# A transformer block on eight cores: the casts of two weight matrices are spread, and drained, at other places of the queue

## The chip, the cores and the metric

The kernel runs on the 8 cores of one Trainium2 chip. Each core does the whole block for its own 1,024 tokens; the cores exchange nothing. The time is that of the slowest core on the device, in microseconds (us). Engines are called as the profile does: PE (TensorE), DVE (VectorE), ACT (ScalarE), POOL (GpSimd), SP (SyncE).

## What is computed

```
x: 2 x 4096 tokens, 4096 wide, float32;  Wq, Wo: 4096 x 4096;  K, V: 8 heads x 8192 keys x 128 (gathered)
def ffn(x):    # 8 low-rank experts, rank 16, routed by a softmax
    scores = 8 * softmax(x @ Wr.T + br)
    low = einsum('bsd,hrd->bshr', x, A)
    return 2 * einsum('bshr,hor,bsh->bso', low, B, scores)
def attn(x):   # 32 query heads, 8 K/V heads, rope on q, no mask
    q = rope(x @ Wq)
    return softmax(q @ K.T / sqrt(128)) @ V @ Wo
x = x + 0.5 * ffn(layernorm(x))
x = x + attn(layernorm(x))
x = x + 0.5 * ffn(layernorm(x))
```

## The kernel before

A core takes its tokens in two chunks of 512 (c = 0 and 1), and the stages of a chunk follow each other: LN, FFN, LN, QT (q with rope), ATT, WO, LN, FFN, STORE. Activations lie transposed in SBUF, 32 tiles of 128 x 512: X in float32, XN and QC in bf16. The program writes one list of instructions for each engine; an engine runs its list in order, and what crosses engines is a semaphore that the later instruction waits for. A DMA belongs to the list of the engine that issues it, and a wait in front of it holds back all that is listed behind it on that engine.

**The casts.** Wq and Wo are float32 in HBM. QT of chunk 0 loads Wq through POOL, which converts to bf16 on the way (L406). The later users, WO of both chunks and QT of chunk 1, read bf16 copies, wob and wqb, that the kernel makes itself, once, in chunk 0. This is `precast_pump` (L448): one call moves one of 128 blocks (64 of Wo first, then 64 of Wq; 128 x 2048 values, 512 KB as bf16). POOL issues a converting load into the single buffer PCB (L458), waiting until the previous block has been written back; SP issues the write to wob or wqb (L464), waiting for that load. The queue `pc_queue` is filled before ATT of chunk 0 (L679, L680). Calls stand in three places: in ATT at every eighth flush of the first 640 (L560; 80 calls), in WO after each of the 32 output blocks (L631; 32 calls), and at the head of STORE until the queue is empty (L635; 16 calls). In chunk 1 the queue is empty and the calls do nothing.

**ATT.** 8 head groups of 4 query heads. For each head, 32 steps of 256 keys: two score matmuls (L511), one exp on ACT (L518), then, two steps later, the flush: row sums (L539) and context (L551). A chunk has 1,024 flushes, 128 a group. K and V of a group lie in SBUF in 4 slabs each. When the fourth head of a group has flushed the last step of a slab (flushes 103, 111, 119 and 127 of the group, counted from 0), POOL issues the loads of that slab for the next group (L472, L479), waiting for PE; the call of a cast, if one is due at that flush, is listed behind them. All calls before a slab's loads in the program stand before them in the POOL list.

**WO.** 32 output blocks of 32 matmuls (L615). Their weights come in halves of 512 KB into WB, issued by ACT (L600), each half waiting until the 16 matmuls on it are done. DVE adds each block to X (L626). The first load also waits for the last cast of Wo.

**LN** has POOL square each tile (L202) after DVE cast it (L198), and PE sums both (L209, L217). **FFN** ends in 32 adds to X on DVE (L349). **STORE** has SP issue 32 stores of X to y (L640), each waiting for its add, and in chunk 0 then 32 loads of chunk 1's X (L649), which all wait for the last store. The next chunk's first cast (L198) waits for all 32 loads.

The lists that the change touches are those of POOL and SP; both hold the casts.

Of the kernel before, what the change touches and what calls it, by code (L numbers as in the profile page):

```python
# [73 lines left out]
def build_program():  # L74
# [35 lines left out]
    with ctx:  # L110
# [334 lines left out]
        pc_queue = []  # L445
        pco_done = {}

        def precast_pump(n=1):  # L448
            for _ in range(n):
                if not pc_queue:  # L450
                    return
                which, blk = pc_queue.pop(0)
                i, hh = blk // 2, blk % 2
                w_d = wo_d if which == "o" else wq_d
                dst_d = wob_d if which == "o" else wqb_d
                osem = sPCOo if which == "o" else sPCOq
                GP.add(
                    (lambda i=i, hh=hh, w_d=w_d: lambda g: g.dma_start(  # L458
                        PCB[:, :].rearrange("p (j m) -> p j m", j=16),
                        w_d.rearrange("(j p) m -> p j m", p=128)  # L460
                        [:, hh * 16:(hh + 1) * 16, i * 128:(i + 1) * 128]))(),
                    waits=[free.get(("pcb",))], inc=sPCI, inc_amt=16)
                v = SY.add(
                    (lambda blk=blk, dst_d=dst_d: lambda s: s.dma_start(  # L464
                        dst_d[blk], PCB[:, :]))(),
                    waits=[(sPCI, sPCI.val)], inc=osem, inc_amt=16)
                free[("pcb",)] = (osem, v)
                pco_done[which] = (osem, v)
# [24 lines left out]
        def emit_ATT(c, po_qt):  # L493
# [32 lines left out]
            def flush_group(item):  # L526
                g, qh, grp, gg, ac_e = item
                h = g * 4 + qh
                cb = 2 + (h % 2)
                lb = 4 + (h % 2)  # L530
                slot = (2 * gg) % NPS
                pe_L = pe_ctx = None
                for t in range(2):
                    j = 2 * grp + t
                    wl = [(sAC, ac_e)]
                    if j == 0:
                        wl.append(bw(lb))
                    pe_L = PE.add(
                        (lambda lb=lb, slot=slot, t=t, j=j: lambda tt: tt.matmul(  # L539
                            BNK[lb], ONES[:, :],  # L540
                            PS4[:, (slot + t) * CH:(slot + t + 1) * CH],
                            start=(j == 0), stop=(j == NK - 1)))(),
                        waits=wl, inc=(sPE if j == NK - 1 else None))
                    wc = [vtv[(g, j // SLAB)]]
                    if j == 0:
                        wc.append(bw(cb))
                    need_inc = (t == 1) and (
                        (qh == 3 and (j % SLAB) == SLAB - 1)
                        or grp == NK // 2 - 1)
                    pe_ctx = PE.add(  # L550
                        (lambda g=g, j=j, slot=slot, t=t, cb=cb: lambda tt: tt.matmul(  # L551
                            BNK[cb], VT[:, j * 128:(j + 1) * 128],
                            PS4[:, (slot + t) * CH:(slot + t + 1) * CH],
                            start=(j == 0), stop=(j == NK - 1)))(),
                        waits=wc, inc=(sPE if need_inc else None))
                    if qh == 3 and t == 1 and (j % SLAB) == SLAB - 1:
                        free[("kvslab", j // SLAB)] = (sPE, pe_ctx)
                        if g + 1 < NG:
                            emit_kv_slab(c, g + 1, j // SLAB, ktv, vtv)
                if flushctr[0] % 8 == 0 and (flushctr[0] % 1024) < 640:  # L560
                    precast_pump(1)
                flushctr[0] += 1
                if grp == NK // 2 - 1:
                    ac_lnl = AC.add(
                        (lambda lb=lb: lambda sc: sc.activation(
                            MB[:, :], BNK[lb], AF.Ln))(),
                        waits=[(sPE, pe_L), free.get(("mb",))], inc=sAC)
                    free[("pb", lb)] = (sAC, ac_lnl)
                    ac_rl = AC.add(lambda sc: sc.activation(  # L569
                        RSD[:, :], MB[:, :], AF.Exp, scale=-1.0),  # L570
                        waits=[(sAC, ac_lnl), free.get(("rsd",))], inc=sAC)
                    free[("mb",)] = (sAC, ac_rl)
                    dv_c = DV.add(
                        (lambda h=h, cb=cb: lambda v: v.tensor_tensor(  # L574
                            tile(QC, h), BNK[cb], RSD[:, :], ALU.mult))(),
                        waits=[(sPE, pe_ctx), (sAC, ac_rl)], inc=sDV)
                    free[("pb", cb)] = (sDV, dv_c)
                    free[("rsd",)] = (sDV, dv_c)
                    dv_ctx[h] = dv_c
# [12 lines left out]
        def emit_WO(c):  # L592
            ctx_all = (sDV, dv_ctx[NH - 1])
            pe_last = None
            for i in range(DT):
                dghalf = []
                for hh in range(2):
                    wsem = sWS0 if hh == 0 else sWS1
                    dg_cb = AC.add(
                        (lambda i=i, hh=hh: lambda sc: sc.dma_start(  # L600
                            WB[:, hh * 2048:(hh + 1) * 2048],
                            wob_d[2 * i + hh]))(),
                        waits=[free.get(("wb", hh)), pco_done.get("o")],
                        inc=wsem, inc_amt=16)
                    dghalf.append((wsem, dg_cb))
                b = i % 2
                pe_o = None
                for j in range(DT):
                    w = []
                    if j == 0:  # L610
                        w = [dghalf[0], ctx_all, bw(b)]
                    elif j == 16:
                        w = [dghalf[1]]
                    pe_o = PE.add(
                        (lambda i=i, j=j, b=b: lambda t: t.matmul(  # L615
                            BNK[b],
                            WB[:, (0 if j < 16 else 2048) + (j % 16) * 128:
                                  (0 if j < 16 else 2048) + (j % 16) * 128 + 128],
                            tile(QC, j), start=(j == 0), stop=(j == DT - 1)))(),
                        waits=w, inc=(sPE if j in (15, DT - 1) else None))  # L620
                    if j == 15:
                        free[("wb", 0)] = (sPE, pe_o)
                free[("wb", 1)] = (sPE, pe_o)
                pe_last = pe_o
                dv_add = DV.add(
                    (lambda i=i, b=b: lambda v: v.tensor_tensor(  # L626
                        tile(X, i), BNK[b], tile(X, i), ALU.add))(),
                    waits=[(sPE, pe_o), free.get(("xrd", i))], inc=sDV)
                free[("pb", b)] = (sDV, dv_add)
                x_state[c][i] = (sDV, dv_add)  # L630
                precast_pump(1)  # L631
            free[("qc_all",)] = (sPE, pe_last)

        def emit_STORE(c):
            while pc_queue:  # L635
                precast_pump(1)
            st_last = None
            for i in range(DT):
                st_last = SY.add(
                    (lambda i=i, c=c: lambda s: s.dma_start(  # L640
                        y_d.rearrange("(i p) t -> p i t", p=128)
                        [:, i, c * CH:(c + 1) * CH],
                        tile(X, i)))(),
                    waits=[x_state[c][i]], inc=sST, inc_amt=16)
            if c == 0:
                ld_last = None
                for i in range(DT):
                    ld_last = SY.add(
                        (lambda i=i: lambda s: s.dma_start(  # L649
                            tile(X, i),  # L650
                            x_d.rearrange("(i p) t -> p i t", p=128)
                            [:, i, CH:2 * CH]))(),
                        waits=[(sST, st_last)], inc=sXL, inc_amt=16)
                for i in range(DT):
                    x_state[1][i] = (sXL, ld_last)

        for c in range(NCH):
# [20 lines left out]
            if c == 0:  # L678
                pc_queue.extend([("o", b) for b in range(2 * DT)])  # L679
                pc_queue.extend([("q", b) for b in range(2 * DT)])  # L680
            emit_ATT(c, po_qt)
            emit_WO(c)
            dv_xn = emit_LN(c)
            emit_FFN(c, dv_xn)
# [92 lines left out]
```

How the kernel before makes its waits and increments, by code:

```python
    def replay(self, eng):  # L63
        for fn, waits, inc, amt in self.ops:
            for s, v in waits:
                eng.wait_ge(s.h, v)
            if fn is None:
                continue
            instr = fn(eng)
            if inc is not None:
                instr.then_inc(inc.h, amt)
```

## Time and profile before

| | us |
|---|---|
| median of 2 runs | 5179.19 |
| the runs | 5139.91, 5218.46 |
| the profiled execution | 5158.56 |
| its span on the slowest core, core 6 | 5157.0 |
| spans of the eight cores | 5090.0 to 5157.0 |

| engine | busy us | share of the span |
|---|---|---|
| PE, matmuls | 4102.5 | 80% |
| ACT | 2346.7 | 46% |
| POOL | 775.5 | 15% |
| DVE | 687.5 | 13% |

The page describes one execution on core 6. Times in rows count from the start of its span. Issuing a DMA is not counted as busy for an engine, though the rows give the issues a duration. "PCB<-wo" names what is written and what is read; "L458" is a line of the kernel; in brackets stands how long the engine sat idle before the instruction and what released it. The granted clock is that of PE, 1.00 for 2.4 GHz; 0.50 is 1.2 GHz. A window's figure is a mean.

### The profile page before, as it was taken

Reading aid. Unit: us, or ns where it says so; the run is one execution under the profiler, and the core shown is the slowest. Engines: PE = TensorE matmul, PEld = TensorE weight load, DVE = VectorE, ACT = ScalarE, POOL = GpSimd, SP = SyncE. Lnnn points to the kernel's source line nnn. Section 1 sums busy time; section 2 is a strip of 40 time slices with the busy share of each in tenths; the row PEclk is TensorE's granted clock in tenths of the full one; section 3 lists DMA queues with packets and bytes.
Section 4 is the critical chain, followed back from the end, with each engine's and each line's share of the span. In section 5 each row is a group of like instructions: output and inputs, shape, how many; then the busy total and the mean of one; then the engine's idle time right before and its main releaser. Section 6 shows DMA issues by size and latency. Waiting matters only on the chain.

```text
span 5157.0 us, 46643 instructions; the slowest of 8 cores (5090.0 to 5157.0 us)
## 1 busy us (share of the span) xinstructions
PE 4102.5 (80%) x17224; PEld 1703.2 (33%) x17224; DVE 687.5 (13%) x937; ACT 2346.7 (46%) x2193; POOL 775.5 (15%) x722
## 2 busy tenths in 40 slices
PE   2556679879789899977851155999999999999985
PEld 0112234334334344432310011444444444444331
DVE  2531110000000000000041164320000000000025
ACT  0000028768577688830000000048888888888000
POOL 4531111111111100100051254000000000000005
PEclk9678889989899999988955556999999999999995
DMA  4167886776776621667516513412022211220432
GB/s 79 17 57 75 80 90 97 103 111 93 104 106 100 89 33 17 99 131 158 149 20 93 163 17 81 140 66 33 9 25 33 33 17 17 33 33 1 142 119 73
DMA packets 616055, 378.54 MB, mean 73 GB/s; under 512 B 549024, under 2 KB 549024, under 8 KB 615840
## 3 DMA queue, kind: packets, MB, share of 16 engines
q0 software_dynamic: 551392, 174.22, 32.8%
q10 hardware_dynamic: 27360, 99.63, 5.8%
q1 hardware_dynamic: 37088, 101.73, 5.2%
q8 instruction: 147, 2.41, 0.2%
q14 instruction: 68, 0.56, 0.0%
HBM read 465.83 MB, written 83.89 MB: 107 GB/s over the span
## 4 chain that ended last, share of the span: by engine, by line
PE 50%; DMA 32%; POOL 8%; issue 5%; ACT 2%; SPq 1%; DVE 1%; POOLq 0%; ACTq 0%; DVEq 0%
DMA PCB<-wo 11%; PE pl L539 11%; PE pc L551 11%; PE psA L615 7%; PE psA L422 7%; PE psA L511 6%; PE psB L511 6%; DMA PCB<-wq 5%; DMA wob<-PCB 5%; DMA WB<-wq 4%; POOL SQr L202 4%; DMA WB<-wob 4%; POOL XN L260 2%; PE pl L217 2%; POOL TTr L256 2%
## 5 line engine op out<-in xcount | busy, mean ns | idle before, releaser
L518 ACT ACTIVATE PS<-psA,CST 128x1024 bf16<-128x1024 f32 x1024 | 1139.8, 1113 | 1064.5 <-PE psA L511 1064.5
L551 PE MATMUL pc<-PS,VT 128*128 128x512 bf16 x4096 | 1566.4, 382 | 4.2 <-DMA VT<-vt 4.2
L539 PE MATMUL pl<-PS,ONES 128*128 128x512 bf16 x4096 | 1567.8, 383 | 0.0
L518 ACT ACTIVATE PS<-psB,CST 128x1024 bf16<-128x1024 f32 x1024 | 1140.6, 1114 | 203.7 <-PE psB L511 196.9
L511 PE MATMUL psA<-QC,KT 128*128 128x512 bf16 x2048 | 618.2, 384 | 147.1 <-DMA KT<-kt 121.2
L422 PE MATMUL psA<-XN,WB 128*128 128x512 bf16 x2048 | 530.5, 420 | 228.3 <-DMA WB<-wq 154.0
L511 PE MATMUL psB<-QC,KT 128*128 128x512 bf16 x2048 | 619.5, 385 | 5.2 <-DVE UR L376 5.2
L551 PEld LDWEIGHTS pc<-PS,VT 128*128 128x128 bf16 x4096 | 403.6, 99 | 501.5 <-issue 26.1
L615 PE MATMUL psA<-QC,WB 128*128 128x512 bf16 x2048 | 493.2, 402 | 92.8 <-DMA WB<-wob 87.2
L539 PEld LDWEIGHTS pl<-PS,ONES 128*128 128x128 bf16 x4096 | 403.7, 99 | 492.7 <-issue 17.7
L238 ACT ACTIVATE G<-RSD,CST 128x512 f32<-128x512 f32 x6 | 4.3, 722 | 1198.9 <-DVE RSD L232 1198.9
L574 DVE TENSOR_TENSOR QC<-pc,RSD 128x512 bf16<-128x512 f32 x64 | 44.3, 691 | 2818.8 <-ACT RSD L569 2818.8
L422 PEld LDWEIGHTS psA<-XN,WB 128*128 128x128 bf16 x2048 | 210.3, 105 | 544.8 <-issue 361.1
L511 PEld LDWEIGHTS psA<-QC,KT 128*128 128x128 bf16 x2048 | 195.6, 98 | 411.4 <-issue 191.6
L615 PEld LDWEIGHTS psA<-QC,WB 128*128 128x128 bf16 x2048 | 204.0, 102 | 382.0 <-issue 184.5
L202 POOL TENSOR_TENSOR SQr<-XN 128x512 bf16<-128x512 bf16 x192 | 210.7, 1097 | 786.8 <-DVE XN L198 623.5
L209 PE MATMUL pl<-XN,ONES 128*128 128x512 bf16 x192 | 120.3, 626 | 249.4 <-DVE XN L198 249.4
L472 POOL DMA_DIRECT2D KT<-kt x64 | 36.0, 562 | 1681.4 <-PE pc L551 1681.4
L511 PEld LDWEIGHTS psB<-QC,KT 128*128 128x128 bf16 x2048 | 202.8, 99 | 254.9 <-issue 19.6
L217 PE MATMUL pl<-SQr,ONES 128*128 128x512 bf16 x192 | 111.9, 583 | 184.5 <-POOL SQr L202 184.5
L458 POOL DMA_DIRECT2D PCB<-wo x64 | 73.2, 1144 | 741.3 <-DMA wob<-PCB 741.3
L458 POOL DMA_DIRECT2D PCB<-wq x64 | 73.2, 1144 | 686.3 <-DMA wqb<-PCB 651.0
(57 smaller groups left out, 1404.9 us busy)
## 6 DMA issues: line engine op xcount, KB each, us to landing
WB<-wob ACTq DMA_DIRECT2D x128, 512.0 KB, 3.4
WB<-wq POOLq DMA_DIRECT2D x66, 512.0 KB, 7.5
KT<-kt POOLq DMA_DIRECT2D x64, 512.0 KB, 5.3
VT<-vt POOLq DMA_DIRECT2D x64, 512.0 KB, 8.9
PCB<-wo POOLq DMA_DIRECT2D x64, 512.0 KB, 7.8
wob<-PCB SPq DMA_DIRECT2D x64, 512.0 KB, 3.1
PCB<-wq POOLq DMA_DIRECT2D x64, 512.0 KB, 8.1
wqb<-PCB SPq DMA_DIRECT2D x64, 512.0 KB, 2.7
```

The costliest lines, as they stand in the source:

```text
L202: (lambda i=i: lambda g: g.tensor_tensor(SQr[:, :], tile(XN, i), tile(XN, i), ALU.mult))(),
L209: (lambda i=i: lambda t: t.matmul(BNK[4], ONES[:, :], tile(XN, i), start=(i == 0), stop=(i == DT - 1)))(),
L217: (lambda i=i: lambda t: t.matmul(BNK[5], ONES[:, :], SQr[:, :], start=(i == 0), stop=(i == DT - 1)))(),
L256: (lambda i=i, sl=sl: lambda e: e.tensor_tensor(tile(TTr, sl), tile(XN, i), MBB[:, :], ALU.subtract))(),
L260: (lambda i=i, sl=sl: lambda e: e.tensor_tensor(tile(XN, i), tile(TTr, sl), RSDB[:, :], ALU.mult))(),
L422: (lambda i=i, j=j, b=b: lambda t: t.matmul(BNK[b], WB[:, (0 if j < 16 else 2048) + (j % 16) * 128: (0 if j < 16 else 2048) + (j % 16) * 1 ...
L458: (lambda i=i, hh=hh, w_d=w_d: lambda g: g.dma_start(PCB[:, :].rearrange("p (j m) -> p j m", j=16), w_d.rearrange("(j p) m -> p j m", p=12 ...
L511: (lambda j=j, b=lo + t, h=h: lambda tt: tt.matmul(BNK[b], KT[:, j * 128:(j + 1) * 128], tile(QC, h), start=True, stop=True))(),
L518: (lambda slot=slot, big=big: lambda sc: sc.activation(PS4[:, slot * CH:(slot + 2) * CH], big[:, :], AF.Exp, bias=CST[:, 0:1], scale=ISQ))(),
L539: (lambda lb=lb, slot=slot, t=t, j=j: lambda tt: tt.matmul(BNK[lb], ONES[:, :], PS4[:, (slot + t) * CH:(slot + t + 1) * CH], start=(j == 0 ...
L551: (lambda g=g, j=j, slot=slot, t=t, cb=cb: lambda tt: tt.matmul(BNK[cb], VT[:, j * 128:(j + 1) * 128], PS4[:, (slot + t) * CH:(slot + t + ...
L615: (lambda i=i, j=j, b=b: lambda t: t.matmul(BNK[b], WB[:, (0 if j < 16 else 2048) + (j % 16) * 128: (0 if j < 16 else 2048) + (j % 16) * 1 ...
```

## The change

Calls of `precast_pump` are moved. In ATT one is made at every eleventh flush, all through the chunk (94 calls in chunk 0, at flushes 0, 11, ... 1023). None is made in WO or in STORE. What is left in the queue, 34 blocks, is drained between ATT and WO: there the program lists 34 loads on POOL and 34 writes on SP, one behind the other. What each call does, the order of the blocks and all other instructions stay as they are. All 128 casts are still made.

```diff
@@ emit_ATT, flush_group
-                if flushctr[0] % 8 == 0 and (flushctr[0] % 1024) < 640:
+                if flushctr[0] % 11 == 0:
                     precast_pump(1)
                 flushctr[0] += 1
@@ emit_WO, the loop over output blocks
                 x_state[c][i] = (sDV, dv_add)
-                precast_pump(1)
             free[("qc_all",)] = (sPE, pe_last)
 
         def emit_STORE(c):
-            while pc_queue:
-                precast_pump(1)
             st_last = None
@@ the loop over chunks
             emit_ATT(c, po_qt)
+            while pc_queue:
+                precast_pump(1)
             emit_WO(c)
```

## Rows read from the trace of the kernel before

**Rows 1.** The core table: span and mean granted TensorE clock

```profile
core 2: 5145.9 us, clock 0.887
...
core 6: 5157.0 us, clock 0.884
```

**Rows 2.** Waits of PE, 690 to 2260: us in total, times, longest

```profile
PE psA L511 <- DMA KT<-kt: 121.2, 20, 16.6
```

**Rows 3.** Score (L511) and WO (L615) matmuls, core 6: ns min/median/max, first and last start

```profile
L511 PE MATMUL psA<-QC,KT x1024: 376/379/634, 728.8 to 2238.8; 128*128 128x512 bf16 x171
...
L615 PE MATMUL psA<-QC,WB x1024: 376/379/634, 2247.9 to 2585.3; 128*128 128x512 bf16 x171
...
L511 PE MATMUL psA<-QC,KT x1024: 376/379/631, 3416.7 to 4764.6; 128*128 128x512 bf16 x171
...
L615 PE MATMUL psA<-QC,WB x1024: 376/379/631, 4772.9 to 5011.8; 128*128 128x512 bf16 x171
```

**Rows 4.** Windows: stretch, length, busy PE, PEld, DVE, ACT, POOL, clock, DMA share, GB/s

```profile
957.00:1092.00 135.00, 134.49 (x620) 60.36 (x619) 2.08 (x3) 116.77 (x109) 13.77 (x13) 1.00 0.62 94
...
1092.00:1160.00 68.00, 41.06 (x149) 15.88 (x148) 0.69 (x1) 28.97 (x27) 11.36 (x12) 0.79 0.91 124
...
2247.00:2480.00 233.00, 164.00 (x580) 64.24 (x581) 12.45 (x18) 0.00 (x0) 19.43 (x17) 0.81 0.77 161
...
3417.00:4765.00 1348.00, 1329.96 (x6128) 597.80 (x6127) 24.61 (x36) 1163.85 (x1084) 47.78 (x56) 1.00 0.18 23
```

**Rows 5.** The POOL queue in order of time: start us, us, instruction, idle before

```profile
957.24 1.15 POOL L458 DMA_DIRECT2D PCB<-wo  x1 [14.60 <-DMA wob<-PCB]
...
1091.95 1.14 POOL L458 DMA_DIRECT2D PCB<-wo  x1 [11.47 <-DMA wob<-PCB]
...
1093.08 0.56 POOL L472 DMA_DIRECT2D KT<-kt  x1
...
1317.61 1.15 POOL L458 DMA_DIRECT2D PCB<-wo  x1 [18.07 <-DMA wob<-PCB]
...
2044.94 0.56 POOL L472 DMA_DIRECT2D KT<-kt  x1 [136.21 <-PE pc L551]
...
2076.84 1.17 POOL L458 DMA_DIRECT2D PCB<-wq  x1
...
2250.68 1.15 POOL L458 DMA_DIRECT2D PCB<-wq  x1 [11.67 <-DMA wqb<-PCB]
...
2469.56 1.15 POOL L458 DMA_DIRECT2D PCB<-wq  x1 [11.46 <-DMA wqb<-PCB]
```

**Rows 6.** DVE at the end of chunk 0, in order of time

```profile
2707.63 1.29 DVE L349 TENSOR_TENSOR X<-psA,X 128x512 f32<-128x512 f32 x2 [0.74 <-PE psA L340]
...
2725.57 1.27 DVE L349 TENSOR_TENSOR X<-psB,X 128x512 f32<-128x512 f32 x2
...
2922.43 17.58 DVE L198 CAST XN<-X 128x512 bf16<-128x512 f32 x32 [195.59 <-DMA X<-x]
```

**Rows 7.** The SP queue at the end of chunk 0

```profile
2871.86 21.82 SPq L640 DMA_DIRECT2D y<-X  x32
```

**Rows 8.** WO of chunk 0: PE timeline, then the chain of waits

```profile
2262.87 9.75 PE L615 MATMUL psA<-QC,WB 128*128 128x512 bf16 x32 [6.27 <-DMA WB<-wob]
...
2276.40 9.81 PE L615 MATMUL psA<-QC,WB 128*128 128x512 bf16 x32 [3.79 <-DMA WB<-wob]
...
2269.24 6.91 DMA WB<-wob
```

**Rows 9.** DMA issues, us to landing: 2247 to 2480, then 4765 to 5012

```profile
WB<-wob ACTq DMA_DIRECT2D x36, 512.0 KB, 5.8
...
WB<-wob ACTq DMA_DIRECT2D x64, 512.0 KB, 3.3
```

**Rows 10.** As rows 3, for core 2, chunk 0

```profile
L511 PE MATMUL psA<-QC,KT x1003: 376/379/634, 747.7 to 2245.7; 128*128 128x512 bf16 x168
...
L615 PE MATMUL psA<-QC,WB x1003: 376/379/634, 2255.0 to 2566.3; 128*128 128x512 bf16 x168
```

## The prediction

> **What bounds the kernel now.** I read the core table first [rows 1]: the core of the page, core 6, is also the slowest, so its trace is the one to add up; core 2 is 11 us behind it and is the second to watch. The page's engine row says PE 80%, ACT 46%, POOL 15%. That average hides two stages in which PE waits, so I went to the waits of PE by stage, then to the POOL queue in order of time, because every step of the change is an instruction of that queue.
>
> In the attention of token chunk 0, PE waits 121.2 us for K slabs, in 20 waits [rows 2]; no such wait exists in chunk 1. The stretch from the first score matmul to the first matmul of WO is 2247.9 - 728.8 = 1519.1 us in chunk 0 and 4772.9 - 3416.7 = 1356.2 us in chunk 1 [rows 3]. The work is the same, so chunk 0 loses 162.9 us: the waits, and about 42 us of slower matmuls behind each of them. The windows show the latter [rows 4]: in 957 to 1092, without a wait, the granted clock is 1.00; in 1092 to 1160, where slabs come late, it is 0.79; in chunk 1 it is 1.00 over 1348 us. The cause is in the POOL queue [rows 5]. From 957.24 to 1091.95 it issues 13 casts of 512 KB with nothing between: 134.71/12 = 11.2 us each, since one buffer (PCB) is loaded, written back and freed before the next can start. Only then, at 1093.08, does it reach the first slab of the next head group. That slab's wait on PE does not show at all: it had been met long before. In groups 6 and 7, which have no casts, the same instruction waits for PE (136.21 us before 2044.94).
>
> The second place is the end of chunk 0. The last FFN add ends at 2725.57 + 1.27 = 2726.8, but the next cast of X starts at 2922.43, after 195.59 us of idle DVE [rows 6]. In between, the SP queue writes back the last 16 casts before it may issue the first y store, at 2871.86 [rows 7]. PE has nothing at all to do there.
>
> **The change part by part.** All of it is worked out on core 6 against the profiled execution, 5158.56 us (span 5157.0 plus 1.6). That execution stands 20.6 us below the median of the two runs shown, 5179.19.
>
> *Attention, cadence 8 to 11.* Before, groups 0 to 4 carry 16 casts each. After, 1024 flushes hold 94 casts (flush 0, 11, ... 1023), 11 or 12 to a group. A flush lasts 1356.2/1024 = 1.32 us. Between the last slab of one group (flush 127) and the first of the next (flush 231) stand 9 or 10 casts: at 11.2 us that is 112 us, and the stretch is 104 flushes or 138 us long. So POOL is waiting for PE when the slab's place comes free. Between two slabs (8 flushes, 10.6 us) stands at most one cast. Beside slab loads a cast takes longer: before the one at 1317.61 POOL waits 18.07 us for the buffer, 20.9 us from cast to cast with the three issues between. Casts at flush 231 and 242 at that price would hold the slab due at flush 255, 31.8 us later, back by 10 us. A slab is used 25 flushes, or 33 us, after it comes free, so that is hidden. I take the whole 162.9 us as gained. Bounds: nothing gained, if the loads themselves and not the queue make slabs late, up to 163 us.
>
> *Store, 16 casts and WO, 32 casts removed.* The issue of the y stores then hangs on the adds alone. The first is ready at 2707.63 + 0.69 = 2708.3. From the first y store to the first cast of X the trace has 2922.43 - 2871.86 = 50.6 us: 32 stores issued in 21.8, a wait for the last, 32 loads. The adds come faster (0.6 us) than SP issues (0.68 us), so this stays 50.6 us and chunk 1 starts at 2758.9: a gain of 163.5 us. If the stores had to wait for the last add it would be 145 us. POOL has no instruction between the FFN's weight loads and the next LN, and no longer holds it back.
>
> *34 casts drained before WO.* Casts and WO run at once, the casts on POOL and SP, the WO loads on ACT. After the last slab (flush 895 by the code) 12 casts from the loop and 34 from the drain stand in the POOL queue: 46, where 32 stood before. In the trace the first of the 32 is issued at 2076.84, 171 us before WO, and 15 go out before WO starts [rows 5]. That leaves 46 - 15 = 31 beside WO instead of 17. From 2250.68 to 2469.56, 16 casts take 218.88 us, 13.68 us each. So the last of 31 is issued 2.8 + 30 x 13.68 = 413 us after WO starts. POOL then is free for the squares of LN.
>
> WO itself is slowed as long as casts run. In 2247 to 2480 the clock is 0.81 and 18 DVE instructions, one a block, stand in 233 us [rows 4]; chunk 1, without casts, needs 5011.8 - 4772.9 = 239 us for all 32 blocks [rows 3]. The chain and the PE timeline show the cycle [rows 8]: PE starts at 2262.87 and again at 2276.40, a load of WB starts at 2269.24 and 2282.84. That is 13.6 us a block, half of it matmuls at the 1.2 GHz level, half a load of 7 us. The median WO load takes 5.8 us beside the casts against 3.3 us alone [rows 9]. With casts to its end, WO takes 15.0 + 30 x 13.6 + 9 = 432 us. It took 2585.3 - 2247.9 = 337.4. WO (432) and the queue (413) end within 20 us of each other, and the later of them counts: a loss of 94 us. Bounds: if WO regains the full clock and a load alone sets the pace, the queue's 413 us count (loss 76); at the 20.9 us that a cast takes at worst beside slab loads, the last is issued at 630 us (loss 292); if casts go at 11.2 us and WO at its own pace, both end by 340 us (no loss). I take the cycle of the rows because they are the same instructions in the same stage.
>
> The Trainium skill bears on this (DMA: Bandwidth & Descriptors, "Queues, rings and completion order"): each DMA engine goes round the queue rows that have work. By it a 3.3 us load beside a cast would take about 6.6 us, and a block with full-clock matmuls 3.5 + 6.6 = 10.1 us; WO would end first and the queue's 413 us would stand. The sum would come out 18 us lower, within my range.
>
> *Sum.* 5157.0 - 162.9 - 163.5 + 94 = 4924.6, with 1.6 around it 4926. Core 2 has 1507.3 us of attention and 311.3 us of WO in chunk 0 [rows 10]. By the same steps it gains 151 and about 164 and loses about 104 (bound by the queue at 415), so it ends near 4935. I predict 4930 us.
>
> **The rivals.**
> *A. Casts beside WO are dearer.* More casts in the same stretch as the WO loads; each 17 us, midway between 13.7 and 20.9. For it: casts slow from 11.2 to 13.7 us as soon as WO runs, and slab loads take them to 20.9. Against it: the 16 casts measured in WO are just this pairing. The last is issued at 513 us, a loss of 175 instead of 94: 5007 us.
> *B. Slab waits stay in part.* If half of the 163 us came from slow loads rather than a late queue, 5010 us. Against it: the rows show slab instructions issued right behind a cast, without a wait of their own, and 33 us of slack.
> *C. The clock falls in dense attention.* The Trainium skill (TensorE: Matmul & The Clock Gate, Part 1) knows a limiter that takes a die below full clock once three of its cores run dense matmuls. As a mechanism of this kernel: attention of chunk 0 without waits keeps PE full on all cores. At the mean clock of the WO window, 0.81, 1329.96 us of PE work would take 312 us more: 5240 us. Against it: chunk 1 is just as dense and has 1.00 over 1348 us [rows 4]; the trace disagrees with that limiter here.
> *D. The other side: slower.* Casts and WO loads starve each other, so that the queue holds LN back. The two gains are 326 us, and the median is 21 us above this execution, so it decides once the last cast is issued 337 + 347 = 684 us after WO starts, from 22.7 us a cast on; at twice the present price, 27.4 us, that is 825 us, a loss of 487 and a time of 5319 us. The dearest spacing in the rows is 20.9 us.
> *E. The backlog is cheaper.* WO runs at near its own pace and casts at 11.2: no loss, 4832 us. Against it: both are slowed in 2247 to 2480.
>
> **How the numbers follow.** My forecast has 0.64, with its own range of 4900 to 4975; A 0.13, B 0.11, C 0.03, D 0.03, E 0.06. The range 4870 to 5030 leaves out C, D, most of E and the tails of A and B, some 0.18 together. About 2% is what a measurement of this kernel can tell from no change, 5076 to 5283 us. Faster by more holds the forecast, A, B and E: 0.93. Within 2%: C and A at its dearest: 0.04. Slower: D, 0.03.
>
> **What would show it.** Right: no K slab waits to speak of in chunk 0's attention and a clock of 1.00 in it; WO of chunk 0 at 400 to 435 us, longer than before; y stores issued while the adds run, and about 32 us from the last add to the cast of X. Wrong: slab waits with the slab instruction issued on time (B); casts over 15 us in WO (A); a long wait of the LN squares behind casts while WO has ended early, by more than 40 us, would mean that the queue alone sets the end.

## The result, and the profile after

| | us |
|---|---|
| forecast | 4930, range 4870 to 5030 |
| median of the changed kernel, 11 runs | 4947.22 (4934.07 to 5269.82) |
| its profiled execution, span on core 4 | 4947.22, 4945.6 |
| median of the kernel before, 10 runs | 5294.02 (5139.91 to 5624.42) |
| ratio, after to before | 0.9595, 95% interval 0.9569 to 0.9621 |

In some runs of every kernel here but e3 the cores of a die are slower at a lower granted clock, and six of the ten runs of the kernel before took 5275 us or more, which is why its median stands so far above the 5179.19 of the first two; the ratio and all comparisons below leave such runs out, and one run each of e1, e2 and e4 remains, two or three of the others. The change is a gain of 4.05%. The forecast, 4926 to 4930 against 5158.56, was a ratio of 0.955 to 0.956, a gain of 4.4 to 4.5%, just outside the interval on the hopeful side. Scaled to the shifted median of before, the ratio gives 0.9595 x 5294.02 = 5080 us, outside the range, which was laid around the one profiled execution, 5158.56. The runs of the changed kernel that are compared took 4934.07 to 4956.07 us.

The core table of the changed kernel; core 4 is the slowest in this execution, and core 6, on which the sum was made, is second [rows 1]. In the other runs compared, cores 0, 2, 4, 6 and 7 take turns as the slowest:

```profile
core 2: 4915.0 us, clock 0.905
...
core 4: 4945.6 us, clock 0.900
...
core 6: 4943.5 us, clock 0.901
```

First score matmul and first and last WO matmul of chunk 0 on core 4 (the page's core; some matmul records are missing, hence x1003):

```profile
L511 PE MATMUL psA<-QC,KT x1003: 376/379/379, 712.3 to 2059.5; 128*128 128x512 bf16 x168
...
L615 PE MATMUL psA<-QC,WB x1003: 376/379/634, 2071.6 to 2486.1; 128*128 128x512 bf16 x168
```

The same on core 6 [rows 3]:

```profile
L511 PE MATMUL psA<-QC,KT x1024: 376/379/379, 747.6 to 2093.0; 128*128 128x512 bf16 x171
...
L615 PE MATMUL psA<-QC,WB x1024: 376/379/634, 2104.5 to 2481.2; 128*128 128x512 bf16 x171
```

Attention on core 6 takes 2104.5 - 747.6 = 1356.9 us where it took 1519.1; WO takes 376.7 where it took 337.4. No K slab wait is left. The windows of core 4 (length, busy time of PE, PEld, DVE, ACT, POOL, clock, DMA share, GB/s) give the attention of chunk 0, WO of chunk 0 and the attention of chunk 1 [rows 4]:

```profile
713.00:2060.00 1347.00, 1321.91 (x6003) 597.36 (x6127) 24.25 (x36) 1162.50 (x1085) 155.31 (x150) 1.00 0.70 98
...
2066.00:2495.00 429.00, 270.67 (x1004) 108.33 (x1025) 29.63 (x55) 0.00 (x0) 33.92 (x30) 0.85 0.74 152
...
3201.00:4548.00 1347.00, 1322.30 (x6003) 597.49 (x6127) 25.13 (x37) 1163.53 (x1084) 47.80 (x56) 1.00 0.18 23
```

Both attentions have clock 1.00. In chunk 0 the DMA engines are busy for 0.70 of the time, and PE's busy time is the same as in chunk 1, where they are busy for 0.18. POOL in order of time, core 4 [rows 5]:

```profile
1865.60 0.56 POOL L472 DMA_DIRECT2D KT<-kt  x1 [19.68 <-PE pc L551]
...
2078.73 1.14 POOL L458 DMA_DIRECT2D PCB<-wq  x1 [14.08 <-DMA wqb<-PCB]
...
2520.25 1.15 POOL L458 DMA_DIRECT2D PCB<-wq  x1 [9.88 <-DMA wqb<-PCB]
...
2521.42 1.05 POOL L202 TENSOR_TENSOR SQr<-XN 128x512 bf16<-128x512 bf16 x1
```

A slab's instruction now waits for PE (19.68 us), as it should. But the last cast is issued at 2520.25, and the first square of LN follows it at once. In the kernel before, the same square on core 6 came 117 us after the last cast there and waited for DVE, that is for the end of WO [rows 5]:

```profile
2586.99 1.08 POOL L202 TENSOR_TENSOR SQr<-XN 128x512 bf16<-128x512 bf16 x1 [116.27 <-DVE XN L198]
```

PE's own row on core 4 says what the wait for POOL costs:

```profile
2481.49 4.99 PE L615 MATMUL psA<-QC,WB 128*128 128x512 bf16 x15 [5.33 <-DMA WB<-wob]
...
2522.73 0.58 PE L217 MATMUL pl<-SQr,ONES 128*128 128x512 bf16 x1 [34.37 <-POOL SQr L202]
```

WO's last matmul of chunk 0 was done at 2486.5. PE made one sum of LN and then stood still for 34.37 us, for a POOL that was queueing casts. The end of chunk 0, SP and then DVE [rows 6, 7]:

```profile
2641.70 21.55 SPq L637 DMA_DIRECT2D y<-X  x32
```

```profile
2640.94 1.29 DVE L349 TENSOR_TENSOR X<-psA,X 128x512 f32<-128x512 f32 x2 [0.74 <-PE psA L340]
...
2658.88 1.27 DVE L349 TENSOR_TENSOR X<-psB,X 128x512 f32<-128x512 f32 x2
...
2698.88 17.58 DVE L198 CAST XN<-X 128x512 bf16<-128x512 f32 x32 [38.72 <-DMA X<-x]
```

The first add is at 2640.94 and the first y store at 2641.70; 38.72 us after the last add the cast of chunk 1 begins, where 195.59 us lay before.

### The profile page after: what moved, and what is told of

Read it like the earlier page. It is cut to its first block, busy times and chain, and to the rows that moved or that the text cites. A ratio compares the mean times of both kernels' runs of the same rounds, so it can differ in the third digit from the quotient of the medians.

```text
span 4945.6 us, 46299 instructions; the slowest of 8 cores (4893.7 to 4945.6 us)
## 1 busy us (share of the span) xinstructions
PE 4051.0 (82%) x16880; PEld 1699.2 (34%) x17224; DVE 680.1 (14%) x937; ACT 2345.3 (47%) x2193; POOL 777.4 (16%) x722
## 4 chain that ended last, share of the span: by engine, by line
PE 61%; DMA 20%; POOL 9%; issue 5%; ACT 3%; DVE 1%; SPq 1%; another core or an unknown queue 0%; POOLq 0%; ACTq 0%; DVEq 0%
PE pc L551 15%; PE pl L539 15%; DMA PCB<-wq 9%; PE psA L511 8%; PE psB L511 8%; PE psA L422 7%; DMA WB<-wq 4%; POOL SQr L202 4%; PE psA L615 4%; DMA wqb<-PCB 3%; POOL XN L260 2%; PE pl L217 2%; POOL TTr L256 2%; ACT PS L518 2%; DMA WB<-wqb 1%
## 5 line engine op out<-in xcount | busy, mean ns | idle before, releaser
L551 PE MATMUL pc<-PS,VT 128*128 128x512 bf16 x4013 | 1522.1, 379 | 4.7 <-DMA VT<-vt 0.3
L539 PE MATMUL pl<-PS,ONES 128*128 128x512 bf16 x4013 | 1522.1, 379 | 4.3
L615 PE MATMUL psA<-QC,WB 128*128 128x512 bf16 x2006 | 498.4, 406 | 170.9 <-DMA WB<-wob 163.3
L511 PE MATMUL psA<-QC,KT 128*128 128x512 bf16 x2006 | 600.1, 379 | 33.6 <-ACT PS L518 31.4
L511 PE MATMUL psB<-QC,KT 128*128 128x512 bf16 x2010 | 601.8, 379 | 7.3 <-DVE UR L376 5.2
L615 PEld LDWEIGHTS psA<-QC,WB 128*128 128x128 bf16 x2048 | 205.3, 103 | 464.2 <-issue 270.3
L202 POOL TENSOR_TENSOR SQr<-XN 128x512 bf16<-128x512 bf16 x192 | 208.7, 1087 | 685.9 <-DVE XN L198 522.5
L511 PEld LDWEIGHTS psA<-QC,KT 128*128 128x128 bf16 x2048 | 196.1, 98 | 286.4 <-issue 59.7
L511 PEld LDWEIGHTS psB<-QC,KT 128*128 128x128 bf16 x2048 | 200.4, 98 | 247.9 <-issue 7.2
```

The costliest lines, as they stand in the source:

```text
L202: (lambda i=i: lambda g: g.tensor_tensor(SQr[:, :], tile(XN, i), tile(XN, i), ALU.mult))(),
L511: (lambda j=j, b=lo + t, h=h: lambda tt: tt.matmul(BNK[b], KT[:, j * 128:(j + 1) * 128], tile(QC, h), start=True, stop=True))(),
L539: (lambda lb=lb, slot=slot, t=t, j=j: lambda tt: tt.matmul(BNK[lb], ONES[:, :], PS4[:, (slot + t) * CH:(slot + t + 1) * CH], start=(j == 0 ...
L615: (lambda i=i, j=j, b=b: lambda t: t.matmul(BNK[b], WB[:, (0 if j < 16 else 2048) + (j % 16) * 128: (0 if j < 16 else 2048) + (j % 16) * 1 ...
```

## The experiments

Stage times below are worked out from the traces in the same way for each kernel: "attention" is from the first score matmul to the first WO matmul of chunk 0, "WO" from its first to its last matmul, "LN starts" the first square (L202) after WO, counted from WO's first matmul, "casts in WO" the casts issued from there to that square, and "STORE" from that square to the first cast of chunk 1; it holds LN and FFN of chunk 0 as well. "Slab waits" are PE's waits for K slabs. Ranges run over the eight cores of the profiled execution.

| | attention | slab waits | WO | LN starts | casts in WO | STORE | profiled, us |
|---|---|---|---|---|---|---|---|
| before | 1480 to 1519 | 82 to 121 | 301 to 337 | 303 to 339 | 16, 17 | 328 to 343 | 5158.56 |
| changed | 1356 to 1361 | 0 | 319 to 415 | 411 to 450 | 31, 32 | 174 to 178 | 4947.22 |
| e1 | 1488 to 1531 | 92 to 135 | 363 to 414 | 430 to 443 | 32, 33 | 175 to 178 | 5118.31 |
| e2 | 1356 to 1363 | 0 to 1.5 | 319 to 344 | 321 to 346 | 16 | 334 to 345 | 5020.20 |
| e3 | 1411 to 1482 | 34 to 84 | 308 to 340 | 310 to 342 | 15 | 172 to 178 | 4956.13 |
| e4 | 1355 to 1358 | 0 | 223 to 226 | 412 to 440 | 31 to 33 | 175 to 177 | 4926.04 |
| e5 | 1355 to 1370 | 0 to 8.6 | 351 to 385 | 353 to 387 | 24 to 26 | 174 to 180 | 4896.05 |
| e6 | 1356 to 1364 | 0 | 334 to 366 | 336 to 368 | 23 to 25 | 177 to 180 | 4876.45 |
| e7 | 1354 to 1356 | 0 | 222 to 224 | 224 to 225 | 0 | 177 to 178 | 4718.07 |

The theory after the first look: the change is two gains that have nothing to do with each other (slabs on time, y stores on time), paid for in one place, where the POOL queue and not WO sets the start of LN. The rivals: one of the gains carries all; or WO's own slowdown is what is paid.

**e1, one part undone: the cadence.** The casts go back to the old places in ATT, 48 are drained.

```diff
-                if flushctr[0] % 11 == 0:
+                if flushctr[0] % 8 == 0 and (flushctr[0] % 1024) < 640:
```

> The changed kernel with its cadence in ATT set back to every eighth of the first 640 flushes; the 48 casts left are drained before WO, none stands in STORE. Theory (two gains that add up, and a POOL queue that sets the start of LN after WO): K slab waits of 80 to 120 us come back and the attention of chunk 0 is 125 to 160 us longer than the changed kernel's 1356; 48 casts instead of 46 behind the last slab delay LN by 2 x 13.9 = 28 us more. About 4947 + 150 + 28 = 5125 us. Rival (the gain of the cadence is small, nearly all came from STORE): about 4975 us.

5118.31 us, 7 below the expectation of the theory and 143 above the rival's. The slab waits are back; PE's wait on core 0, the slowest:

```profile
PE psA L511 <- DMA KT<-kt: 134.8, 19, 19.8
```

On core 0 that makes an attention of 1531 us. So the cadence, with the two casts fewer that it leaves to the drain, is worth 171 us of the 211 between the two profiled executions. The early drain alone, which is this kernel against the kernel before, is worth 40 us between the two profiled executions: STORE falls by 153 to 166 us a core, but LN starts 103 to 136 us later, because 48 casts and not 32 stand behind the last slab. The stages point the same way; the totals alone would not show it, since single runs of one kernel lie up to some 60 us apart.

**e2, another part undone: 16 casts back at the head of STORE.**

```diff
-            while pc_queue:
+            while len(pc_queue) > 16:
                 precast_pump(1)
             emit_WO(c)
@@ emit_STORE
+            while pc_queue:
+                precast_pump(1)
             st_last = None
```

> The changed kernel with only 18 casts drained before WO and the last 16 put back at the head of STORE. Theory: behind the last slab stand 30 casts instead of 46, 15 of them beside WO; the queue is through about 200 us into WO and WO's own end (about 320 us) starts LN, 110 us earlier than the changed kernel's 430; STORE gives back 163 us. About 4947 - 110 + 163 = 5000 us. Rival (casts beside WO cost little): 5110 us. Rival (STORE was worth little): 4850 us.

5020.20 us against the theory's 5000. The SP queue of its slowest core, core 3, has the 16 write-backs ahead of the first y store, which is issued here:

```profile
2730.20 21.82 SPq L639 DMA_DIRECT2D y<-X  x32
```

and the DVE after it:

```profile
2782.86 17.58 DVE L198 CAST XN<-X 128x512 bf16<-128x512 f32 x32 [203.69 <-DMA X<-x]
```

The idle time of 203.69 us is back at the size that it had in the kernel before, 195.59 [rows 6]. STORE gives back 159 to 167 us, as said; LN starts at 321 to 346 us instead of 411 to 450. The expected 320 for the end of WO was met by the best cores and missed by 20 us on core 3, which sets the time.

**e3, a cadence of nine.**

```diff
-                if flushctr[0] % 11 == 0:
+                if flushctr[0] % 9 == 0:
```

> The changed kernel with a cast at every ninth flush: 114 in ATT, 14 drained, so 28 behind the last slab instead of 46. Theory: LN starts at WO's own end, about 310 us after its start instead of 430 (gain 115); a group's 14.2 casts need about 10.7 x 11.2 + 3.5 x 17 = 180 us of a group's 169, the lag grows by 11 us a group and passes the 33 us of slack after three, so 30 to 50 us of slab waits come back. About 4947 - 115 + 45 = 4877 us. Rival (eleven was needed to keep the slabs on time at all, waits as in the old cadence): 4950 us or more. Rival (no waits at nine): 4832 us.

4942.08 and 4956.13 us in two runs: no gain, a miss of 72 us, and by the time alone the rival's 4950. But LN starts as early as the theory said on the best core (310 to 342), and the slab waits, 34 to 84 us, are less than the old cadence's, so the cause is not quite the rival's either. The slab waits are what the theory undersized. On core 0:

```profile
PE psA L511 <- DMA KT<-kt: 83.9, 17, 9.1
```

On POOL there, the first slab instructions of two groups are issued with no wait of their own, so the queue is late from the first group on:

```profile
862.59 0.56 POOL L472 DMA_DIRECT2D KT<-kt  x1
...
1053.58 0.56 POOL L472 DMA_DIRECT2D KT<-kt  x1
```

190.99 us lie between them, where PE's own time for a group is about 169. The expectation had 180, with an estimate of 17 us for a cast beside slab loads. And a wait costs more than its length: with 83.9 us of waits, attention is 1481.7 - 1357.4 = 124 us longer than in the changed kernel, as in the kernel before, where 121.2 us of waits went with 162.9 us [rows 2, 3]. Of the second part I saw only that the clock is below 1.00 where slabs are late [rows 4].

**e4, WO's weights loaded up to three halves ahead.** Two more half buffers lie in a part of XN that nothing uses between QT and the next LN. The edit in short:

```diff
-            WB[:, hh * 2048:(hh + 1) * 2048], wob_d[2 * i + hh]      # waits for half n - 2
+    wsl = [WB[:, 0:2048], WB[:, 2048:4096], XN[:, 8192:10240], XN[:, 10240:12288]]
+            wsl[n % 4], wob_d[n]                                     # n = 2 * i + hh, waits for half n - 4
```

> The changed kernel with four half buffers for WO's weights instead of two (two of them in XN, unused there), so that loads run up to three halves ahead of PE; casts as in the changed kernel. Theory (the POOL queue alone sets the start of LN): WO of chunk 0 ends 50 to 100 us earlier, at 250 to 330 us, but the squares of LN still wait behind the 46th cast; same time, 4930 to 4965 us. Rival (WO's loads set the pace of the stage): 40 us or more faster. Rival (the denser loads take DMA time from the casts): casts at 15 us or more while WO runs, slower.

This is the run that separates the queue from WO. The matmuls of WO in chunk 0 end 226 us after they start (2093.3 to 2319.1 on core 0; the row is that of the halves in XN), and the window 2100 to 2300 has clock 1.00, with casts beside them all the time:

```profile
L625 PE MATMUL psA<-QC,XN x512: 379/379/379, 2102.6 to 2319.1; 128*128 128x512 bf16 x171
```

```profile
2100.00:2300.00 200.00, 197.61 (x916) 89.45 (x915) 20.07 (x29) 0.00 (x0) 13.75 (x13) 1.00 0.94 213
```

And LN starts about where it did, 412 to 440 us after WO's start. The POOL queue of core 0:

```profile
2532.05 1.15 POOL L458 DMA_DIRECT2D PCB<-wq  x1 [9.59 <-DMA wqb<-PCB]
...
2533.21 1.05 POOL L202 TENSOR_TENSOR SQr<-XN 128x512 bf16<-128x512 bf16 x1
```

WO is done at 2319 and LN waits for the last cast until 2533. The whole time is 4926.04, 21 us less than the changed kernel's profiled execution and 8 us less than its fastest run. The traces show where most of it lies: WO of chunk 1, which has no casts, also fell, from 239 to 242 us to 222 to 223. I had left that out of the expectation, and had put WO of chunk 0 at 250 us or more. The 93 to 191 us that WO of chunk 0 gained are worth nothing.

The DMA issues of this window say something about the price of a load, with the median time to landing last:

```profile
XN<-wob ACTq DMA_DIRECT2D x28, 512.0 KB, 5.8
...
PCB<-wq POOLq DMA_DIRECT2D x13, 512.0 KB, 9.9
```

A WO load takes 5.8 us beside casts and 3.3 alone [rows 9], and WO does not feel it when it is three halves ahead. So the slow WO of both kernels was not a lack of bandwidth (the DMA engines move 213 GB/s here, 152 in the changed kernel's WO). It was a load that could only start when PE had finished the half, and a granted clock of 0.85 with the gaps that this leaves, where it is 1.00 here. How the lost time divides between the loads and the clock, no run separates. That a load takes 5.8 and not 3.3 us beside casts agrees with the Trainium skill (DMA: Bandwidth & Descriptors, "Queues, rings and completion order"), by which an engine takes turns among its queue rows.

**e5, a cadence of ten.** The same line as e3, with % 10.

> The changed kernel with a cast at every tenth flush: 103 in ATT, 25 drained, 38 behind the last slab instead of 46. Theory (one cadence between nine, where slab waits of 34 to 84 us came back, and eleven, where there are none): a group's 12.8 casts need about 10.3 x 11.2 + 2.5 x 17 = 158 us of a group's 169, so no slab waits; 23 casts stand beside WO, LN starts 310 to 345 us after WO's start instead of 410 to 450. About 4860 us. Rival (slab waits grow smoothly with the cadence): half of those at nine, 4910 us.

4896.05 and 4923.84 us: 23 to 51 us below the changed kernel's 4947.22, not the 87 expected. The ratio to the kernel before is 0.9443, but its interval, 0.9296 to 0.9589, overlaps that of cadence eleven, so the gain over eleven is likely and not shown. The slab waits are gone as the theory said, all but 5 us on cores 2 and 4 and 8.6 on core 0, which is also the slowest:

```profile
PE psA L511 <- DMA KT<-kt: 8.6, 2, 4.3
```

and the end of its POOL queue:

```profile
2450.63 1.15 POOL L458 DMA_DIRECT2D PCB<-wq  x1 [12.82 <-DMA wqb<-PCB]
...
2482.53 1.08 POOL L202 TENSOR_TENSOR SQr<-XN 128x512 bf16<-128x512 bf16 x1 [30.75 <-DVE XN L198]
```

Here WO and not the queue sets the end: POOL is free at 2452, 344 us after WO's start, and waits 30.75 us for DVE, that is for WO. That was the step missed in the expectation. With 24 to 26 casts beside it, WO takes 351 to 385 us, more than the queue, whose last cast is issued after 316 to 343.

**e6, a second cast buffer, cadence eleven.** Block n goes to PCB or to 4 tiles of XN in turn; each buffer has its own semaphores.

```diff
+                b = pcn[0] % 2
-                        PCB[:, :].rearrange(...)      waits=[free.get(("pcb",))], inc=sPCI
+                        pbuf[b].rearrange(...)        waits=[plast[b]], inc=sPI[b]
```

> The changed kernel, cadence eleven, with a second cast buffer (4 tiles of XN, unused from QT to the next LN), so that one block is loaded while the other is written back. Theory (a cast's 11.2 us are the sum of load and write-back, one behind the other): 8 to 9 us a cast in ATT, 10 to 12 beside WO; about 26 casts stand beside WO, LN starts at WO's end or close behind, 320 to 360 us after WO's start. About 4865 us. Rival (the DMA engines are the limit of a cast, not the order): 11 us as with one buffer, 4947 us.

4871.91 and 4876.45 us, close to the expectation of 4865; the ratio to the kernel before is 0.9374, interval 0.9242 to 0.9505, and so clear of the changed kernel's. The POOL queue of core 3 in WO:

```profile
2109.85 1.14 POOL L470 DMA_DIRECT2D PCB<-wq  x1 [19.68 <-DMA wqb<-PCB]
...
2129.45 1.14 POOL L470 DMA_DIRECT2D PCB<-wq  x1 [17.04 <-DMA wqb<-PCB]
...
2323.89 1.15 POOL L470 DMA_DIRECT2D XN<-wq  x1
...
2449.28 1.08 POOL L204 TENSOR_TENSOR SQr<-XN 128x512 bf16<-128x512 bf16 x1 [124.23 <-DVE XN L200]
```

Two casts, one in each buffer, take 19.6 us (2109.85 to 2129.45); the mean over the cores is 9.2 to 10.1 each, where one buffer needs 13.2 to 14.2. The queue is through at 2325, and the squares wait 124.23 us for WO. So a good part of a cast's price was the order of load and write-back in one buffer, and not a limit of the DMA engines. WO itself stays slow, and now it sets the end.

**e7, all of it: two cast buffers, a cast at every eighth flush to the end of ATT, WO loaded ahead.**

> Two cast buffers, a cast at every eighth flush all through ATT (128, so nothing is left to drain), and the four half buffers for WO's weights of e4. Theory (slabs were late because of their place in the queue, not because of the bytes that casts move; LN waited for the queue): 16 casts a group at 8 to 9 us are through before the slab's turn, so slab waits of 0 to 30 us in chunk 0 although the casts are denser than ever; WO takes 216 us and LN starts at 218. About 4947 - 207 - 24 + 15 = 4730 us. Rival (the bytes make the slabs late): waits of 80 us or more, 4850 us or more.

Three runs took 4718.07 to 4723.33 us, 0.9083 of the kernel before, interval 0.8956 to 0.9210. The expectation was 4730. All 128 casts run inside the attention, at the cadence of eight of the kernel before and now in all eight groups, more than in any other kernel here. The windows of core 2, attention and WO of chunk 0:

```profile
732.00:2086.00 1354.00, 1331.24 (x6144) 598.52 (x6142) 25.29 (x37) 1164.71 (x1088) 191.93 (x183) 1.00 0.88 124
...
2090.00:2300.00 210.00, 210.00 (x971) 95.03 (x970) 20.74 (x30) 0.00 (x0) 0.00 (x0) 1.00 0.45 150
```

The DMA share of the attention is 0.88, PE is busy for 1331 of 1354 us at full clock, and no slab is waited for. The POOL queue shows the slab's instruction waiting for PE, the last cast issued 50 us before WO begins, and LN's first square waiting for DVE alone:

```profile
1883.13 0.55 POOL L487 DMA_DIRECT2D KT<-kt  x1 [24.63 <-PE pc L566]
...
2035.98 1.15 POOL L470 DMA_DIRECT2D XN<-wq  x1 [0.26 <-issue]
...
2311.34 1.08 POOL L204 TENSOR_TENSOR SQr<-XN 128x512 bf16<-128x512 bf16 x1 [274.21 <-DVE XN L200]
```

This settles the first question: slabs were late in the kernel before through their place behind casts that took 11.2 us each in a chain, not through the bytes the casts move. At the same cadence of eight slabs were late with one buffer, in the kernel before and in e1; with two buffers none is. It also beats both kernels. Loads ahead with one cast buffer and the best cadence were not tried, so how much of e7 each part needs is open.

## Why the prediction was right in its mechanisms, and which term failed

*Attention: right.* 162.9 us forecast on core 6, 1519.1 - 1356.9 = 162.2 measured. Clock 1.00, no slab waits, slab instructions waiting for PE. e1 shows the gain on its own, e7 its cause. What the sum did not carry is that core 6 had the longest attention before; the others gained 123 to 146 us.

*STORE: right.* 163.5 forecast. On core 6, from LN's first square to chunk 1's cast, 335.4 us became 174.1, a gain of 161.3. The first cast comes 38.7 us after the last add on core 4, where I had about 32.

*The step that failed: the term for the 34 drained casts, a loss of 94 us.* It went wrong twice. First, it let WO's own end, 432 us, start LN and took the queue's 413 for as good as equal. WO took 319 to 415 us over the cores and was not the later of the two on any; LN waited behind the queue for 23 to 108 us more. Second, the queue was priced with one core's cast and one core's count. On core 6 that was close:

```profile
2524.11 1.15 POOL L458 DMA_DIRECT2D PCB<-wq  x1 [9.33 <-DMA wqb<-PCB]
2525.28 1.05 POOL L202 TENSOR_TENSOR SQr<-XN 128x512 bf16<-128x512 bf16 x1
```

The last cast was issued 419.6 us after WO's start, against the forecast 413, and LN started at 420.8; the loss is 81.7. On core 4, which ended last, casts beside WO took 14.24 us each instead of 13.68 (2520.25 - 2078.73 over 31), and 32 and not 31 of them stood there. LN started at 449.8 instead of 323.3: a loss of 126.5 where the sum had 94. Over the eight cores the price is 13.2 to 14.2 us, and with 31 casts in a row half a us is 16 us.

*Why WO's end was wrong.* I took 32 blocks at 13.6 us from two blocks of the trace [rows 8]. They were of the slow kind, with part of the matmuls at the 1.2 GHz level; even the window beside them has 18 blocks in 233 us, 12.9 each [rows 4]. How many blocks are slow differs from core to core. Core 4 has a clock of 0.85 in WO and takes 415 us, core 0 has 0.94 and takes 319:

```profile
2071.00:2390.00 319.00, 245.40 (x1024) 101.09 (x1024) 21.45 (x31) 0.00 (x0) 26.25 (x23) 0.94 0.85 177
```

That is 10.0 us a block on core 0, the 10.1 that the prediction had for full-clock matmuls, with the queue as what counts. The forecast also named this outcome, LN's squares behind casts with WO done more than 40 us before, as a sign of being wrong; five of the eight cores show it.

*The rest of the sum.* On core 4 the span was 5127.5 before. Attention takes 136.1 off, STORE 164.1, the queue adds 126.5; it entered attention 20 us earlier, which no part of the change explains, and chunk 1's stages up to attention took 9 us longer. That makes 4943, with 4945.6 measured. On core 6, 5157.0 - 162.2 - 161.3 + 81.7 gives 4915, with 4943.5 measured: it entered attention 19 us later, and chunk 1's stages up to attention took 8 us longer. The entry to attention lies between 704 and 748 us over the cores of both profiled executions, and the sum held it still.

So it is in part luck that 4930 stands only 17 us from 4947.22. On core 4 the attention gained 27 us less than in the sum and the queue cost 32 more, and a span that was 29.5 us shorter to begin with and the earlier entry made up most of it. As a gain, the forecast was too large by about a tenth, 4.4 to 4.5% for 4.05%. A shift of 20 us in a stage that the change leaves alone is as large as that error.

*The rivals.* A (17 us a cast) was too dear at 14.2. B fell: no slab waits. C, the limiter of the Trainium skill (TensorE: Matmul & The Clock Gate, Part 1), does not show in these traces: clock 1.00 over 1347 us of dense attention on the page's core, in chunk 0 and chunk 1, and 1.00 on all eight cores in the window 750 to 2060. D fell, and E with it, though e6 gets below E's cast price by a second buffer.

## What to carry to other kernels

In this kernel background DMAs issued from an engine's in-order queue cost what they held back in the queue; their bytes cost the attention nothing (e7), nor a WO whose loads ran ahead (e4). Price such a queue from the last point at which it was on time, as count times interval, and compare that with what the next instruction on it needs. Spread such work so that each stretch between two deadlines has slack at the price a transfer has beside other traffic, and take the price from several cores, not from one. Where the transfers wait for one another through one buffer, try a second buffer, even a borrowed one: here it was worth more than any of the cadences tried (nine, ten, eleven).

## What was not expected of the hardware

K slab waits go with a loss of about 1.3 to 1.6 times their length over the cores of before, e1 and e3: 121.2 us of waits with 162.9 us of longer attention, 83.9 us with 124, and the granted clock was 0.79 in a stretch with late slabs [rows 4]. I did not test whether the clock is all of the surplus.

With 0.94 of the DMA time busy and 213 GB/s (e4, WO), matmuls whose weights were three halves ahead ran at full clock; with 0.74 and 152 GB/s and weights one half ahead, the changed kernel's WO took 1.9 times as long on core 4. The DMA share by itself said nothing about which of the two would wait.
